# Attention and a mixture of experts on one core: the values before the transpositions in each steady turn

## The chip, the cores and the metric

The kernel runs on one core of a Trainium2 chip. The metric is the device time of one execution in microseconds. All computation is in one launch; nothing runs on other cores.

## What is computed

Eight batches of 128 tokens with 256 features pass through one block. Cut to what matters, the reference is:

```python
x = x + attention(layernorm(x), ctx, ctx, length)    # 8 batches, 8 * 16 = 128 "heads x 16" rows, see below
x = x + moe(layernorm(x))                            # 8 experts, capacity 128, plus a shared expert

def attention(q, k, v, length):      # q, k, v: (8, 128, 256); the 128 rows are 8 heads of 16
    s = SCALE * log(length)          # one factor for each batch
    attn = softmax(s * einsum('bhdq,bhdk->bhqk', q, k))
    return einsum('bhqk,bhdk->bhdq', attn, v)

def moe(x):                          # 1024 tokens
    probs = softmax(x @ Wg); e = argmax(probs); gate = probs[e]
    # the first 128 tokens of each expert in order are kept
    out = gate * ((silu(x @ W1[e]) * (x @ W3[e])) @ W2[e])
    return out + (silu(x @ sw1) * (x @ sw3)) @ sw2
```

## The kernel before

There are 64 heads in all, eight for each of eight batches. The attention runs as a software pipeline of "turns", t = 0 to 32 (STEADY = 33), written out by hand in the same order for each engine. Each engine executes its own list in order and waits on semaphores. A turn handles two heads.

TensorE's part of turn t was, before the change:

- **Values**, one half of a group (weigh_values, L1110). A group m is four heads. Its eight matmuls multiply the exponentials pt with the values vext and add into the PSUM bank O; half c=0 starts the sums, c=1 ends them and raises valued. Group m had its halves in turns 2m+10 and 2m+11. Two groups make a batch; the first half of a batch's first group waits for o_copied, as it overwrites O.
- **Scores** (L1070) of heads 2t and 2t+1, up to turn 31, whose row maxima VectorE takes (nm, L578), interleaved with **shifted scores** (L1094) of heads 2(t-7) and 2(t-7)+1. These are the scores again, transposed and with the maxima subtracted; ScalarE takes their exponentials (pt, L843). A score of head n waits for the maximum of head n-3, which has the same bank.
- **Transpositions**, at most one kind in a turn, through the bank X, which they share in a fixed order (x_free). In turns 4b+4 the maxima of batch b (turn_maxima, L1079); in turns 4b+14 the attention output of batch b from osum (turn_output, L1124), waiting for o_copied; in turns 4b+15 its way back after the division (turn_back, L1136), waiting for scaled; in turns 21, 25, 29 the normed tokens (turn_tokens, L1147).

From turn 12 on, there is a transposition in each turn save 13 and 17. Turns 12, 16, 20, 24, 28 and 32 have the maxima.

ScalarE in a turn: if it is turn 4b+13, copy_output (osum, L849: O to SBUF after valued, raises o_copied); then the first exponential; then, in turns 4b+4, maxima_rows (mrow, L836, waits for the maxima's transposition and lets SP reload them into qz by two small DMAs); or high_tokens (xhi, L859) after a token transposition; then the second exponential; then token_rstd (rstd, L855) of the second layer norm.

VectorE in a turn: two maxima (L578), then one of scale_output (rinv L586, att L591), add_attention (xs, L600), token statistics (st, L605) or low_tokens (xlo, L616). In turn 14 it also takes the statistics of the last two query batches (st, L535). GpSimd does the token norm (mrs L440, rk L443) after rstd and splits weights (L450 to L465). The expert splitting starts in turn 32 and is followed by token_norm(4).

Behind the loop the order is written out: half (11, 1) of the values, the shifted scores of heads 52 to 55, turn_tokens(3), values (12, 0), turn_output(5), values (12, 1), shifted scores of 56 to 59, turn_back(5), values 13, turn_tokens(4), shifted scores of 60 to 63, turn_output(6) and so on into the shared expert and the experts.

Of the kernel before, what the change touches and what calls it, by code (L numbers as in the profile page):

```python
# [46 lines left out]
NG = NH // 4  # L47
# [11 lines left out]
LAG = 7  # L59
# [27 lines left out]
END = TURNS + LAG  # L87


def turns(offset, *last):  # L90


    return [4 * b + offset for b in range(B - len(last))] + [END + n for n in last]
# [1 line left out]

WEIGH = [(2 * m + LAG + 3, 2 * m + LAG + 4) for m in range(NG - 1)] + [(END, END)]
OUT_COPY, OUT_TURN, OUT_SCALE = turns(LAG + 6, 1), turns(LAG + 7, 4), turns(LAG + 7, 5)
OUT_BACK, OUT_ADD = turns(LAG + 8, 6), turns(LAG + 8, 7)  # L100
SHIFTED = 5
# [17 lines left out]
def shifted_bank(n):  # L119

    return NS + n % NS if n < FOURS else FOURS_BANKS[(n - FOURS) % len(FOURS_BANKS)]


def banks_last_head(n):

    return next((k for k in range(n - 1, -1, -1) if shifted_bank(k) == shifted_bank(n)), None)
# [40 lines left out]
def block_kernel(nc, x, ctx_in, lens, wg, w1, w3, w2, sw1, sw3, sw2, consts, out):  # L167
    with ExitStack() as es:
# [148 lines left out]
        def ring_pass(n, size):  # L317

            return n // size + 1
# [687 lines left out]
        def _(pe):  # L1007
# [17 lines left out]
            def unread(t):  # L1025

                if t in (4, 6, 7):
                    pe.wait_ge(nm_row, 1)
                if t == 9:
                    pe.wait_ge(nm_row, 2)  # L1030
                unread_rows(UNREAD.get(t, 0))
# [3 lines left out]
            def turn_values(n):  # L1035

                if n == 0:
                    pe.wait_ge(ld_cst, 16)
                else:
                    pe.wait_ge(v_copied, n)  # L1040
                for b in range(2 * n, 2 * n + 2):
                    pe.wait_ge(ld_ctx[chunk_of[b]], 16)
                    for c in range(2):
                        k = 2 * (b % 2) + c
                        mm = nc.tensor.transpose(O[:, k * P:(k + 1) * P], cs[:, b, c * P:(c + 1) * P], ident)
                mm.then_inc(v_turned, 1)

            def place(n):

                b, i = divmod(n, H)  # L1050
                first = ROWS * (HEADS[i] // 2)
                return b, HEADS[i] % 2, slice(first, first + ROWS)

            def scores(n, u):

                b, half, rows = place(n)
                scores_bank = bank[n % (2 * NS) if n < FIRST else n % NS]
                if n % H == 0 and u == 0:
                    if b < EAGER:
                        pe.wait_ge(k_eager, 2 * b + 1)  # L1060
                        pe.wait_ge(q_eager, b + 1)
                    else:
                        pe.wait_ge(k_made, 2 * (b - EAGER + 1))
                        pe.wait_ge(q_made, 2 * (b + 1) - EAGER)
                if n % H == 2 and u == 0 and b < EAGER:
                    pe.wait_ge(k_eager, 2 * (b + 1))
                    pe.wait_ge(q_made, b + 1)
                if n >= 2 * NS and u == 0:
                    pe.wait_ge(maxed, n - 2 * NS + 1 if n < FIRST + NS else n - NS + 1)
                mm = nc.tensor.matmul(scores_bank[:, u * D:(u + 1) * D], qz[rows, b, half, u * P:(u + 1) * P],  # L1070
                                      kz[rows, b, half, :], start=True, stop=True)
                if u == 1:
                    mm.then_inc(scored, 1)

            def turn_maxima(b):
                pe.wait_ge(maxed, H * (b + 1))
                x_free("maxima", b)
                for u in range(2):
                    mm = nc.tensor.transpose(X[0:H, u * P:(u + 1) * P], nm[:, b % 2, u, :], ident)  # L1079
                mm.then_inc(nm_turned, 1)  # L1080

            def shifted_scores(n, c):

                b, half, rows = place(n)
                if n < NS and c == 0:
                    pe.wait_ge(maxed, FIRST - NS + n + 1)
                if n % H == 0 and c == 0:
                    pe.wait_ge(ld_m[b % 2], 32 * ring_pass(b, 2))
                last = banks_last_head(n)
                if last is not None and c == 0:  # L1090
                    pe.wait_ge(exped, last + 1)
                if n >= FOURS and shifted_bank(n) < NS and c == 0:
                    pe.wait_ge(maxed, NH)
                mm = nc.tensor.matmul(bank[shifted_bank(n)][:, c * D:(c + 1) * D], kz[rows, b, half, c * P:(c + 1) * P],  # L1094
                                      qz[rows, b, half, :], start=True, stop=True)
                if c == 1:
                    mm.then_inc(shifted, 1)

            def weigh_values(m, c):

                b, first = divmod(m, 2)
                pe.wait_ge(exped, 4 * m + 4)
                if m == 0:
                    pe.wait_ge(v_copied, B // 2)
                if first == 0 and b >= 1:
                    pe.wait_ge(o_copied, b)
                for i in range(4):
                    h = HEADS[4 * first + i]
                    g, j = divmod(h, 4)
                    mm = nc.tensor.matmul(O[32 * j:32 * j + 32, g * D:(g + 1) * D], vext[:, b, c, h, :],  # L1110
                                          pt[:, m % NPT, i, c * D:(c + 1) * D],
                                          start=(c == 0), stop=(c == 1), skip_group_check=True)
                if c == 1:
                    mm.then_inc(valued, 1)
# [92 lines left out]
                mm.then_inc(pos_done, 1)  # L1207

            for t in range(STEADY):
                for m in range(NG):  # L1210
                    for c in range(2):
                        if t == WEIGH[m][c]:
                            weigh_values(m, c)
                if t < LAG and t % 2 == 0:
                    first_half, heads = range(2), range(2 * t, min(2 * t + 4, 2 * LAG))
                    if t == 0:
                        for u in range(2):
                            for n in first_half:
                                scores(n, u)
                        heads = range(2, 4)  # L1220
                    for u in range(2):
                        for n in heads:
                            scores(n, u)
                for part in range(2):
                    for k in range(2):
                        if LAG <= t < TURNS:
                            scores(2 * t + k, part)
                        if 0 <= t - LAG < TURNS:
                            shifted_scores(2 * (t - LAG) + k, part)
                if t == MROW[0]:  # L1230
                    turn_maxima(0)
                if t in VALUES:
                    turn_values(VALUES.index(t))
                if t in UNREAD:
                    unread(t)
                for when, work in ((MROW[1:], turn_maxima), (OUT_TURN, turn_output), (OUT_BACK, turn_back),
                                     (TTURN, turn_tokens)):
                    if t in when:
                        work(when.index(t) + (1 if work is turn_maxima else 0))

            def four_shifted(n):

                for part in range(2):
                    for k in range(4):
                        shifted_scores(n + k, part)
# [77 lines left out]
                                          start=(c == 0), stop=(c == FC - 1))  # L1323
                mm.then_inc(e_down, 1)

            weigh_values(11, 1)
            four_shifted(52)
            turn_tokens(3)
            weigh_values(12, 0)
# [72 lines left out]
```

## Time and profile before

| | |
|---|---|
| median of 3 runs | 153.0 us (152.81 to 153.4) |
| the profiled execution | 153.0 us, span 151.1 us |
| mean granted clock of TensorE | 0.991 |
| busy, share of the span | TensorE 139.9 us (93%), VectorE 99.3 (66%), ScalarE 82.1 (54%), GpSimd 67.9 (45%) |
| scores L1070, shifted scores L1094, values L1110 | 34.6, 34.6, 19.8 us busy |

The span goes from the first to the last instruction; the rest of the time lies around it. Busy time counts overlapping matmuls once in the engine's total. The end of a matmul in the trace is modelled, so groups are best measured from start to start. A turn of the loop takes about 2 us, a cycle of four turns 8.2 us; the loop ends at about 71 us.

### The profile page before, as it was taken

What the parts mean: (1) busy time and instruction counts of PE and PEld (TensorE: products, weight loads), DVE (VectorE), ACT (ScalarE), POOL (GpSimd) and SP (SyncE); (2) the same over time, 40 slices, a digit from 0 to 9 for tenths busy, and PEclk for the clock granted to TensorE, in tenths of its full rate; (3) what the DMA queues carried; (4) which work ended last, traced back from release to release, by engine and by line L of the source; (5) the groups of instructions that cost most, each with busy time, mean ns of one, the idle gap of its engine ahead of it and who ended that gap; (6) DMA issues with size and microseconds to landing.
All of it is one profiled execution on the core that took longest, in us unless ns stands there. A gap on an engine that the chain in (4) does not pass through costs nothing.

```text
span 151.1 us, 3413 instructions
## 1 busy us (share of the span) xinstructions
PE 139.9 (93%) x1254; PEld 95.4 (63%) x1254; DVE 99.3 (66%) x232; ACT 82.1 (54%) x179; POOL 67.9 (45%) x100
## 2 busy tenths in 40 slices
PE   7799999998999999999887999999999999999930
PEld 2365564554554555554443677688999999999720
DVE  0589896778888888887225346877673487774220
ACT  3444275674858676776876357544503676662300
POOL 7116739401850506349992000276600588467250
PEclk9999999999999999999999999999999999999996
DMA  3993454444171700000530099722465622212110
GB/s 70 345 357 118 119 174 143 152 143 146 36 259 39 242 7 5 0 8 0 157 131 4 2 305 323 237 105 70 160 196 156 175 77 80 69 42 91 35 63 35
DMA packets 15825, 18.42 MB, mean 122 GB/s; under 512 B 1981, under 2 KB 15078, under 8 KB 15809
## 3 DMA queue, kind: packets, MB, share of 16 engines
q1 hardware_dynamic: 14368, 14.98, 31.5%
q0 software_dynamic: 1152, 2.97, 6.0%
q10 hardware_dynamic: 288, 0.26, 0.6%
q8 instruction: 10, 0.16, 0.5%
q14 instruction: 7, 0.05, 0.1%
HBM read 14.12 MB, written 4.21 MB: 121 GB/s over the span
## 4 chain that ended last, share of the span: by engine, by line
PE 83%; DVE 4%; DMA 4%; issue 3%; ACT 2%; POOL 1%; SPq 0%; ACTq 0%; POOLq 0%; DVEq 0%
PE bank L1070 20%; PE bank L1110 11%; PE bank L1321 6%; PE bank L1174 6%; PE bank L1175 6%; PE bank L1297 5%; PE bank L1296 5%; PE bank L1262 4%; PE bank L1094 4%; PE bank L1022 3%; PE bank L1124 3%; DMA xs<-in_x 2%; PE bank L1136 2%; PE bank L1079 2%; PE bank L1308 2%
## 5 line engine op out<-in xcount | busy, mean ns | idle before, releaser
L578 DVE TENSOR_REDUCE nm<-bank 128x2 f32<-128x512 f32 x64 | 40.9, 686 | 10.0 <-PE bank L1070 9.5
L843 ACT ACTIVATE pt<-bank 128x512 f32<-128x512 f32 x64 | 35.6, 597 | 17.4 <-PE bank L1094 17.3
L1070 PE MATMUL bank<-kz,qz 32*128 32x256 f32 x256 | 34.6, 400 | 0.9 <-DVE qz L555 0.9
L1094 PE MATMUL bank<-qz,kz 32*128 32x256 f32 x256 | 34.6, 400 | 0.0
L1070 PEld LDWEIGHTS bank<-kz,qz 32*128 32x128 f32 x256 | 21.9, 184 | 13.3 <-DVE nm L578 5.8
L1094 PEld LDWEIGHTS bank<-qz,kz 32*128 32x128 f32 x256 | 21.6, 184 | 1.7 <-ACT pt L843 1.0
L1110 PE MATMUL bank<-pt,vext 128*32 128x256 f32 x256 | 19.8, 390 | 0.1
L502 POOL DMA_INDIRECT expert_rows<-rk,idx_s x8 | 8.7, 1088 | 19.5 <-DVE idx_s L655 17.7
L415 POOL TENSOR_SCALAR qz<-xs,rs,mrs 128x256 f32<-128x256 f32 x14 | 7.7, 561 | 20.0 <-DVE mrs L549 20.0
L517 POOL DMA_INDIRECT xs<-out,rk x8 | 9.9, 1235 | 12.0 <-DMA out<-xs 9.8
L524 POOL DMA_INDIRECT out<-xs,rk x8 | 8.2, 1020 | 8.8 <-DVE xs L741 4.4
L1022 PE MATMUL bank<-onesb 128*128 128x512 bf16 x34 | 10.7, 452 | 1.0 <-POOL onesb L409 1.0
L1110 PEld LDWEIGHTS bank<-pt,vext 128*32 128x32 f32 x256 | 5.4, 108 | 6.8 <-issue 5.2
L440 POOL TENSOR_SCALAR mrs<-mv,rstd 128x1 f32<-128x1 f32 x6 | 1.6, 259 | 16.6 <-ACT rstd L855 16.6
L616 DVE TENSOR_TENSOR xlo<-bank,xhi 128x256 fp32r<-128x256 f32 x8 | 3.4, 421 | 7.0 <-ACT xhi L859 7.0
L465 POOL TENSOR_TENSOR ew<-wraw,ew 128x352 fp32r<-128x352 f32 x8 | 7.5, 932 | 0.7
L968 ACT ACTIVATE late<-bank 128x352 f32<-128x352 f32 x8 | 3.7, 464 | 7.3 <-PE bank L1297 7.3
L735 DVE TENSOR_TENSOR qz_rest<-bank,late 128x352 f32<-128x352 f32 x8 | 4.2, 520 | 5.1 <-ACT late L968 5.1
L1321 PE MATMUL bank<-wraw,kz_rest 128*128 128x256 f32 (+1 forms) x30 | 7.4, 381 | 0.0
L1022 PEld LDWEIGHTS bank<-onesb 128*128 128x128 bf16 x34 | 3.4, 112 | 5.9 <-issue 3.7
L1262 PE MATMUL bank<-shi,hThi 128*128 128x256 f32 (+1 forms) x24 | 7.0, 290 | 0.0
L1262 PE MATMUL bank<-shi,hTlo 128*128 128x256 f32 (+1 forms) x24 | 6.8, 282 | 0.0
(153 smaller groups left out, 301.1 us busy)
## 6 DMA issues: line engine op xcount, KB each, us to landing
wraw<-in_w SPq DMA_DIRECT2D x10, 352.0 KB, 3.4
wlate<-in_w SPq DMA_DIRECT2D x6, 352.0 KB, 4.4
wraw<-in_w SPq DMA_DIRECT2D x10, 128.0 KB, 3.5
expert_rows<-zero SPq DMA_DIRECT2D x1, 1032.0 KB, 6.7
out<-xs SPq DMA_DIRECT2D x8, 128.0 KB, 2.1
xs<-in_x SPq DMA_DIRECT2D x3, 256.0 KB, 5.1
cs<-in_ctx SPq DMA_DIRECT2D x3, 256.0 KB, 5.3
wlate<-in_w SPq DMA_DIRECT2D x6, 128.0 KB, 4.4
```

The costliest lines, as they stand in the source:

```text
L502: nc.gpsimd.indirect_dma_start(xd_dram, bass.IndirectOffsetOnAxis(ap=idx_s[:, b:b + 1], axis=0), x2[:, b, :], None, bounds_check=E * C - 1 ...
L517: nc.gpsimd.indirect_dma_start(res[:, e, :], None, out_rows, number(e), bounds_check=B * P - 1, oob_is_err=False).then_inc(gathered[e], 16)
L578: nc.vector.tensor_reduce(nm[:, b % 2, :, place], scores_bank[:].rearrange("p (u c) -> p u c", u=2), AX_X, ALU.max, negate=True).then_inc( ...
L843: nc.scalar.activation(pt[:, g % NPT, n % 4, :], bank[shifted_bank(n)][:], ACT.Exp).then_inc(exped, 1)
L1022: nc.tensor.matmul(X[:].rearrange("p (n c) -> p n c", c=P), onesb[:], onesb[:].unsqueeze(1).broadcast_to([P, 4, P]), start=True, stop=True)
L1070: mm = nc.tensor.matmul(scores_bank[:, u * D:(u + 1) * D], qz[rows, b, half, u * P:(u + 1) * P], kz[rows, b, half, :], start=True, stop=True)
L1094: mm = nc.tensor.matmul(bank[shifted_bank(n)][:, c * D:(c + 1) * D], kz[rows, b, half, c * P:(c + 1) * P], qz[rows, b, half, :], start=Tru ...
L1110: mm = nc.tensor.matmul(O[32 * j:32 * j + 32, g * D:(g + 1) * D], vext[:, b, c, h, :], pt[:, m % NPT, i, c * D:(c + 1) * D], start=(c == 0 ...
L1174: nc.tensor.matmul(u1, weights(part, S1 + f * P, F + WG, c, n1), tokens, start=a, stop=z)
L1175: mm = nc.tensor.matmul(u3, weights(part, S3 + f * P, F, c, n3), tokens, start=a, stop=z)
L1262: mm = nc.tensor.matmul(base_bank[b % 2][:, 0:D], hpart[0:rows, half, f, j * P:(j + 1) * P], part[0:rows, S2 + f * D:S2 + (f + 1) * D], st ...
L1321: mm = nc.tensor.matmul(y_bank[(e + 1) % 2][:, 0:D], hTe[0:rows, e % 2, c * P:(c + 1) * P], down_at[e][c][0:rows], start=(c == 0), stop=(c ...
```

## The change

The half of the values stands behind the scores of a turn and ahead of its transposition, in place of ahead of the scores. Its turn is one earlier: group m has its halves in turns 2m+9 and 2m+10. In the stream of TensorE's instructions each half so changes places with the transposition (and, in turn 9, with the two unread matmuls) that stood ahead of it. Group 11's second half moves from behind the loop into turn 32. The program of every other engine stays as it is.

```diff
-WEIGH = [(2 * m + LAG + 3, 2 * m + LAG + 4) for m in range(NG - 1)] + [(END, END)]
+WEIGH = [(2 * m + LAG + 2, 2 * m + LAG + 3) for m in range(NG - 4)]
@@
             for t in range(STEADY):
-                for m in range(NG):
-                    for c in range(2):
-                        if t == WEIGH[m][c]:
-                            weigh_values(m, c)
                 if t < LAG and t % 2 == 0:
...
                             scores(2 * t + k, part)
                         if 0 <= t - LAG < TURNS:
                             shifted_scores(2 * (t - LAG) + k, part)
+                for m, halves in enumerate(WEIGH):
+                    for c in range(2):
+                        if t == halves[c]:
+                            weigh_values(m, c)
                 if t == MROW[0]:
                     turn_maxima(0)
@@
-            weigh_values(11, 1)
             four_shifted(52)
             turn_tokens(3)
```

## Rows read from the trace of the kernel before

**Rows 1.** The page, chain that ended last, share of the span by engine.
```profile
PE 83%; DVE 4%; DMA 4%; issue 3%; ACT 2%; POOL 1%; SPq 0%; ACTq 0%; POOLq 0%; DVEq 0%
```

**Rows 2.** Windows: length, busy us of PE, PEld, DVE, ACT, POOL, granted clock, DMA.
```profile
45.64:53.86 8.22, 8.22 (x111) 4.44 (x108) 6.93 (x14) 5.70 (x13) 2.23 (x4) 1.00 0.40 132
...
70.28:83.81 13.53, 11.46 (x142) 5.83 (x141) 5.12 (x15) 10.51 (x26) 9.30 (x15) 1.00 0.25 82
```

**Rows 3.** Timeline of TensorE, turns 20 to 22: start us, length us, what.
```profile
45.64 0.38 PE L1079 MATMUL bank<-cst,nm 128*8 128x128 f32 x2
45.95 0.64 PE L1110 MATMUL bank<-pt,vext 128*32 128x256 f32 x8
46.52 0.48 PE L1070 MATMUL bank<-kz,qz 32*128 32x256 f32 x1
...
47.60 0.44 PE L1147 MATMUL bank<-cst,rk 128*128 128x128 f32 x2
47.97 0.64 PE L1110 MATMUL bank<-pt,vext 128*32 128x256 f32 x8
```

**Rows 4.** Timeline of ScalarE in the same turns.
```profile
46.26 0.34 ACT L836 COPY mrow<-bank 8x256 f32<-8x256 f32 x1
46.51 0.58 ACT L843 ACTIVATE pt<-bank 128x512 f32<-128x512 f32 x1
47.00 0.56 ACT L849 COPY osum<-bank 128x512 f32<-128x512 f32 x1
```

**Rows 5.** Timeline of all engines, turn 4.
```profile
13.59 0.39 PE L1079 MATMUL bank<-cst,nm 128*8 128x128 f32 x2
...
14.01 0.36 ACT L836 COPY mrow<-bank 8x256 f32<-8x256 f32 x1 [1.77 <-PE bank L1079]
```

**Rows 6.** Timeline of all engines, from turn 13 into turn 14.
```profile
29.79 0.48 PE L1070 MATMUL bank<-kz,qz 32*128 32x256 f32 x1
...
30.27 0.56 ACT L849 COPY osum<-bank 128x512 f32<-128x512 f32 x1
...
30.97 0.42 PE L1110 MATMUL bank<-pt,vext 128*32 128x256 f32 x4
```

**Rows 7.** Timeline of VectorE, turn 14.
```profile
32.70 1.29 DVE L578 TENSOR_REDUCE nm<-bank 128x2 f32<-128x512 f32 x2 [0.46 <-PE bank L1070]
33.91 0.74 DVE L535 BATCH_NORM_STATS2 st<-xs 128x6 f32<-128x256 f32 x2
```

**Rows 8.** Timeline of all engines, turn 15.
```profile
35.04 0.42 DVE L591 TENSOR_TENSOR att<-bank,rinv 128x256 f32<-128x256 f32 x1
...
35.39 1.28 DVE L578 TENSOR_REDUCE nm<-bank 128x2 f32<-128x512 f32 x2
...
35.52 0.44 PE L1136 MATMUL bank<-cst,att 128*128 128x128 f32 x2 [0.46 <-DVE att L591]
...
36.46 0.48 PE L1070 MATMUL bank<-kz,qz 32*128 32x256 f32 x1
```

**Rows 9.** Timeline of all engines, start of turn 18.
```profile
40.17 0.48 PE L1070 MATMUL bank<-kz,qz 32*128 32x256 f32 x1
...
40.33 0.48 PE L1070 MATMUL bank<-kz,qz 32*128 32x256 f32 x1
```

**Rows 10.** Timeline of all engines, behind the loop.
```profile
71.61 0.56 ACT L849 COPY osum<-bank 128x512 f32<-128x512 f32 x1
...
72.82 0.37 ACT L859 CAST xhi<-bank 128x256 fp32r<-128x256 f32 x1
...
73.22 0.42 DVE L616 TENSOR_TENSOR xlo<-bank,xhi 128x256 fp32r<-128x256 f32 x1 [1.91 <-ACT xhi L859]
```

**Rows 11.** Timeline of all engines, token norms of GpSimd and who waits.
```profile
66.04 0.26 POOL L440 TENSOR_SCALAR mrs<-mv,rstd 128x1 f32<-128x1 f32 x1 [4.32 <-ACT rstd L855]
...
77.95 0.44 PE L1147 MATMUL bank<-cst,rk 128*128 128x128 f32 x2 [0.51 <-POOL rk L443]
```

**Rows 12.** The page, DMA issues: KB each, median us to landing.
```profile
out<-xs SPq DMA_DIRECT2D x8, 128.0 KB, 2.1
```

## The prediction

> **What bounds the kernel now.** I read four views in this order. The chain that ended last is mostly TensorE [rows 1], so the question is where TensorE waits. The windows over a cycle of four turns show it busy without a gap (8.22 of 8.22 us, turns 20 to 23), while ScalarE has 5.70 us of work there and VectorE 6.93 [rows 2]. In the stretch behind the loop it idles 2.07 of 13.53 us. TensorE's timeline gives the length of each group of a turn from start to start: scores 1.08 us (46.52 to 47.60), maxima 0.31, values 0.57, token transposition 0.37 [rows 3]. These lengths add up in any order: values follow directly on scores in turns 9 to 12 now, at the same 0.57. So swapping groups that never wait is worth nothing. What can move the time is a wait that appears or goes. ScalarE's timeline of the same turns shows the order that matters: mrow (row of maxima), an exponential, then osum (the copy of O), back to back [rows 4].
>
> **What moves.** No instruction, semaphore or DMA is added or removed. Each half of the values in turns 10 to 32 moves ahead of the transpositions in the turn before it. So in every turn with a transposition, that transposition starts 0.57 us later against the scores, and the values start earlier by its length.
>
> **The new wait.** turn_maxima (L1079) runs in turns 4b+12. The second half of group 2b+1 used to follow it and now precedes it. Freeing it early doesn't help: copy_output(b) stands in ScalarE's program behind maxima_rows and one exponential, and maxima_rows waits for the transposition. The next values, group 2b+2, restart O and wait for that copy (o_copied). They used to come after the next scores and that turn's transposition; now they come right after the scores. With M the end of the maxima's transposition:
> - mrow starts at M+0.02 (13.98 to 14.01 in turn 4, where ScalarE had nothing else) [rows 5]. Now it is held until 46.26 by the exponential before it, though M is 46.02.
> - From there 0.25 to the exponential and 0.49 to osum, whose length is 0.56 [rows 4]. It ends at M+1.32.
> - osum's end at 30.83 releases values at 30.97, so 0.14 more [rows 6]: M+1.46.
> - TensorE starts the next scores at M-0.07 (fill and drain overlap: 45.95 against 46.02) and is through with them at M+1.01 [rows 3].
>
> So it waits 0.45 us. Both ends: if the exponential is not in the way or the restart overlaps, 0.30; if transfer times are longer, 0.60. I take 0.45, worked from the nearest rows. Behind the waiting values stand the turn's transposition and the next scores, so VectorE and ScalarE starve with it; neither is late by itself, since each had slack.
>
> **The sum, turn by turn.** Turns 9 to 12 keep their times (no transposition before the maxima of turn 12).
> - Turn 13: wait 0.45, against one of 0.10 now, since turn 13 has no transposition and values start at 30.97 where scores end 1.08 after 29.79. +0.35.
> - Turn 14: now the second head of the scores waits for VectorE's reduction of the turn before, a stagger of 0.16 as in turn 18 (40.17 to 40.33 [rows 9]). The later turn hides it. -0.16, running +0.19.
> - Turn 15: here the swap pays. TensorE idles 0.46 before turn_back(0) [rows 8], which follows VectorE's chain of two maxima, statistics and att that starts with 32.70 [rows 7]. That chain starts 0.36 later, so turn_back goes at 35.88; but the values, 0.57 us, are now done before it. The scores of turn 16 start at 36.25 instead of 36.46. Running -0.21.
> - Turn 16: VectorE is late next. Its pair of maxima from 35.39 [rows 8] moves to 35.75, the first is free after 0.61 and 0.14 more, 36.50. Stagger 0.25, running +0.04.
> - Turn 17: as turn 13, +0.35. Turn 18: stagger gone, -0.16. Running +0.23.
> - Turns 21, 25, 29: these now have a token transposition (0.37) that covers the copy, so the whole 0.45 is new. +1.36, running +1.6 us.
> - Behind the loop ScalarE's order is mrow, exponential, osum, exponential, xhi. It starts at the later M: osum 71.99 instead of 71.61 on the old clock, xhi 72.99 instead of 72.82, then xlo (73.22) and turn_output(5) [rows 10]. +0.17.
>
> Sum +1.77 us. Two covers to check. The reload of the maxima through SP starts 0.35 us later against the turn and is due three turns on, about 4 us after mrow; the SP copies of the outputs land in 2.1 us [rows 12]. Price nothing; only a landing above 4 us would count. GpSimd's token norm waits for rstd [rows 11], whose cause, xhi, is late by 0.57 more than the 0.29 that TensorE's wait and drain already give, so its splitting of expert weights starts about 2.0 us late. turn_tokens(4) waits 0.51 us for it now (77.95) [rows 11] and comes about 0.2 later than the rest, but turn_output(6) waits for ScalarE's chain of osum(6), rstd, an exponential and xhi(4), so that is absorbed. Lost cover would cost 0.2 us. From there everything hangs in one chain on TensorE, so the shift reaches the end.
>
> The profiled execution took 153.0 us with a span of 151.1, the median is also 153.0. 151.1 + 1.8 + 1.9 around the span gives 154.8 us.
>
> **A rule against the row.** The new waits start with a weight load. In the row, TensorE begins again only behind the wait: the values start 0.14 after osum's end [rows 6], and their group of eight then takes the full 0.64, fill included. The Trainium skill (TensorE: Matmul & The Clock Gate, Architectural detail) says that the queue can pull weight loads ahead of matmuls in flight. By it the first load would be done in the wait, and each of five restarts would save the fill of 0.07 at most, for 154.4 us; the rows show no such thing after a semaphore wait. The sum goes by the rows.
>
> **Rivals.**
> - Not slower (0.10): the copy of O is in time. Then the wait of turns 13 to 29 is 0 and only the hidden stall of turns 15 and 16 counts. By the same steps the scores of turn 16 end 0.3 us earlier, and the late VectorE keeps it there: 152.7 us. For it speaks that valued now comes earlier, when ScalarE is idle half of some turns. It decides where osum ends before M+0.87, 0.45 earlier than I work out; against it speaks ScalarE's fixed order [rows 4].
> - Order costs (0.06): transpositions between values and scores lose the overlap of 0.07 that each change of group has now, in 19 turns: +1.3, 156.1 us. The groups behind the loop, values into turn_back, show no such loss.
> - Clock (0.02): the granted clock is 1.00 in the cycles and also in the stretch with 2.07 us of idle [rows 2], the upper of the two levels (2.4 GHz). If five new gaps brought it down to 1.2 GHz, a turn of 2.05 us of TensorE work would take up to twice as long, and five such turns cost 10 us: 165 us. The page named above has this rule under A second HAM failure mode: frequent micro-idles between groups of matmuls let the clock swing. No row here shows it, the wait of 0.46 before turn_back(0) included.
> - Something unseen that leaves the time where it was (0.02).
>
> **The numbers.** My forecast has 0.80. Its own range follows from the wait's ends, five times 0.15 either way: 154.0 to 155.6. The range for 8 in 10 reaches to the neighbours: 153.5 to 156.0. Within 0.5% (0.77 us, about what a measurement tells from no change) lie 0.07 of the first rival, 0.02 of my own low end and the unseen 0.02; faster by more is 0.03 of the first rival, should the tail gain as well. Slower: 0.78 + 0.06 + 0.02, so 0.86.
>
> **What would show it.** Right: TensorE idle of some 0.4 us before values (L1110) in turns 13, 17, 21, 25 and 29, with osum (L849) as releaser or just ended; the 0.46 before L1136 in turn 15 shrunk to 0.1; cycles of 8.67 instead of 8.22 us; the stretch behind the loop longer by 0.2. Wrong: cycles of 8.2 (the copy is in time), waits before L1079, L1136 or L1147 in the steady turns (transpositions late in themselves), waits before L1094 for the reload, or a granted clock under 1.00.

## The result and the profile after

The changed kernel takes 154.91 us in the median (154.82 to 155.06, 4 runs), the kernel before 153.09 us (4 runs); the ratio is 1.0121, 95% interval 1.0109 to 1.0133. The change makes the kernel 1.2% slower. The profiled execution has a span of 153.0 us, 1.9 more than before, with a granted clock of 0.986.

First, three rows of the changed kernel's waits, of TensorE's matmuls alone (engine, what waited, for whom: us in total, times, longest us):

```profile
PE bank L1110 <- ACT osum L849: 2.1, 5, 0.4
...
PE bank L1147 <- POOL rk L443: 0.8, 1, 0.8
...
PE bank L1147 <- DVE xs L600: 0.6, 1, 0.6
```

The page's chain, which answers to [rows 1], passes less through TensorE and more through ScalarE and GpSimd:

```profile
PE 76%; POOL 8%; ACT 5%; issue 4%; DMA 2%; DVE 1%; SPq 0%; ACTq 0%; POOLq 0%; DVEq 0%
```

Of the waits, the first row has no counterpart before the change: five waits of TensorE for the copy of O, 2.1 us together. The other two are behind the loop and were there before (0.51 and 0.61 us). The last one has not grown. Now TensorE's timeline in turns 20 to 22, which answers to [rows 3], and ScalarE's, which answers to [rows 4]:

```profile
45.81 0.64 PE L1110 MATMUL bank<-pt,vext 128*32 128x256 f32 x8
46.38 0.38 PE L1079 MATMUL bank<-cst,nm 128*8 128x128 f32 x2
46.70 0.48 PE L1070 MATMUL bank<-kz,qz 32*128 32x256 f32 x1
...
48.26 0.64 PE L1110 MATMUL bank<-pt,vext 128*32 128x256 f32 x8 [0.42 <-ACT osum L849]
48.83 0.44 PE L1147 MATMUL bank<-cst,rk 128*128 128x128 f32 x2
```

```profile
46.80 0.36 ACT L836 COPY mrow<-bank 8x256 f32<-8x256 f32 x1 [0.26 <-PE bank L1079]
47.07 0.58 ACT L843 ACTIVATE pt<-bank 128x512 f32<-128x512 f32 x1
47.56 0.56 ACT L849 COPY osum<-bank 128x512 f32<-128x512 f32 x1
```

Read the two together. The values of turn 20 are through at 46.45, yet osum, which needs only them, starts at 47.56. ScalarE first sits idle for 0.26 us waiting for the maxima's transposition, which ends at 46.76. mrow follows at 46.80, then an exponential, then osum. osum ends at 48.12 and the values start 0.14 later. TensorE's list has nothing else that it may do. The same row with the same 0.42 stands at 31.26, 39.92, 56.97 and 65.67 (turns 13, 17, 25, 29).

The windows of one cycle show what this costs, and that the work is the same (columns as in [rows 2]):

```profile
45.50:54.20 8.70, 8.28 (x111) 4.46 (x106) 7.01 (x15) 5.71 (x13) 2.23 (x4) 1.00 0.38 124
54.20:62.90 8.70, 8.28 (x110) 4.45 (x106) 7.01 (x15) 5.71 (x13) 3.23 (x6) 1.00 0.01 3
```

A cycle of four turns has become 8.70 us instead of 8.22, at the upper clock level throughout.

Turn 15 is where the swap pays. TensorE's timeline, answering to [rows 8]:

```profile
35.13 0.64 PE L1110 MATMUL bank<-pt,vext 128*32 128x256 f32 x8
35.81 0.44 PE L1136 MATMUL bank<-cst,att 128*128 128x128 f32 x2
36.18 0.48 PE L1070 MATMUL bank<-kz,qz 32*128 32x256 f32 x1
...
36.41 0.48 PE L1070 MATMUL bank<-kz,qz 32*128 32x256 f32 x1
```

turn_back(0) still waits for att, but 0.11 us from start to start (35.13 and 0.57 for the values make 35.70; it starts at 35.81). Before the change the same reckoning gives 0.52 (33.92 and 1.08 make 35.00; it starts at 35.52 [rows 8]). The values fill the time. The stagger in turn 16, the time by which the second head's scores start behind the first head's (36.18 to 36.41), takes back 0.23.

Behind the loop, all engines, answering to [rows 10] and [rows 11]:

```profile
73.67 0.56 ACT L849 COPY osum<-bank 128x512 f32<-128x512 f32 x1
...
74.62 0.34 ACT L859 CAST xhi<-bank 128x256 fp32r<-128x256 f32 x1
...
75.00 0.42 DVE L616 TENSOR_TENSOR xlo<-bank,xhi 128x256 fp32r<-128x256 f32 x1 [2.04 <-ACT xhi L859]
...
80.02 0.44 PE L1147 MATMUL bank<-cst,rk 128*128 128x128 f32 x2 [0.81 <-POOL rk L443]
...
81.64 0.63 PE L1124 MATMUL bank<-cst,osum 128*128 128x128 f32 x4
```

turn_output(5) starts at 75.57, where it started at 73.79 before. Ahead of it, values (12, 0) start 0.49 us after turn_tokens(3) (73.88 to 74.37) instead of 0.37, as they too need O copied; turn_output(5) waits longer than that for xlo, so this costs nothing by itself.

How the delay grows, from the starts of the same group in both timelines. The changed kernel's profiled execution enters turn 12 0.10 us earlier (it is as early already at the first scores, 6.83 against 6.92 us, long before the change), so 0.10 is added to each difference.

| start of | before | after | delay + 0.10 | by the prediction |
|---|---|---|---|---|
| scores of turn 14 | 31.54 | 31.83 | 0.39 | 0.35 |
| scores of turn 16 | 36.46 | 36.18 | -0.18 | -0.21 |
| scores of turn 17 | 38.42 | 38.36 | 0.04 | 0.04 |
| scores of turn 18 | 40.17 | 40.49 | 0.42 | 0.39 |
| scores of turn 19 | 42.55 | 42.72 | 0.27 | 0.23 |
| scores of turn 30 | 64.97 | 66.61 | 1.74 | 1.60 |
| shifted scores of head 52 | 71.16 | 72.80 | 1.74 | 1.60 |
| shared expert, first matmul | 83.81 | 85.59 | 1.88 | 1.77 |

From the last row to the end of the span the changed kernel takes 67.41 us and the kernel before 67.29. These 0.12 us were not traced to a cause; they happen to make up for the 0.10 of the start, so the spans differ by 1.9 as well.

### The profile page after: what moved, and what is told of

Read it like the earlier page. It is cut to its first block, busy times and chain, and to the rows that moved or that the text cites. A ratio compares the mean times of both kernels' runs of the same rounds, so it can differ in the third digit from the quotient of the medians.

```text
span 153.0 us, 3413 instructions
## 1 busy us (share of the span) xinstructions
PE 140.4 (92%) x1254; PEld 95.5 (62%) x1254; DVE 99.6 (65%) x232; ACT 82.2 (54%) x179; POOL 67.5 (44%) x100
## 4 chain that ended last, share of the span: by engine, by line
PE 76%; POOL 8%; ACT 5%; issue 4%; DMA 2%; DVE 1%; SPq 0%; ACTq 0%; POOLq 0%; DVEq 0%
PE bank L1070 16%; PE bank L1110 9%; PE bank L1321 6%; PE bank L1174 6%; PE bank L1262 6%; PE bank L1175 5%; PE bank L1296 5%; PE bank L1297 5%; POOL ew L465 4%; PE bank L1022 3%; DMA xs<-in_x 2%; PE bank L1124 2%; ACT pt L843 2%; POOL ew L463 2%; PE bank L1094 2%
## 5 line engine op out<-in xcount | busy, mean ns | idle before, releaser
L465 POOL TENSOR_TENSOR ew<-wraw,ew 128x352 fp32r<-128x352 f32 x8 | 7.5, 933 | 0.7
L1262 PE MATMUL bank<-slo,hThi 128*128 128x256 f32 (+1 forms) x24 | 6.8, 282 | 0.0
```

The lines of the kernel that those rows point to most:

```text
L465: nc.gpsimd.tensor_tensor(elo[e][:, a:z], whole[e][:, a:z], ehi[e][:, a:z].bitcast(F32), ALU.subtract).then_inc(ew_lo_pool, 1)
L1262: mm = nc.tensor.matmul(base_bank[b % 2][:, 0:D], hpart[0:rows, half, f, j * P:(j + 1) * P], part[0:rows, S2 + f * D:S2 + (f + 1) * D], st ...
```

## The experiments

Each ratio is against the kernel before the change, run on the same chip in the same rounds. The first four ran on one chip. The maxima first, ScalarE's best order on the kernel before and the two with the statistics ran on a second, where the kernel before scattered from 153.04 to 154.10 us; this widens their intervals. GpSimd's norm and both gains at once ran on a third, the copy first on the kernel before on a fourth. Many of the differences here are as small as the intervals. Where a timeline is compared instead, starts are counted from the scores of turn 12 (27.83 before the change, 27.73 after it).

**ScalarE's copy ahead of mrow.** TensorE's list is that of the changed kernel; the copy leaves the start of the next turn for the maxima turn itself.

```diff
-                if t in OUT_COPY:
-                    copy_output(OUT_COPY.index(t))
                 if 0 <= t - LAG < TURNS:
                     exponentials(2 * (t - LAG))
+                if t in MROW[2:]:
+                    copy_output(MROW.index(t) - 2)
                 if t in MROW[1:]:
                     maxima_rows(MROW.index(t))
```

> The changed kernel, with ScalarE's copy of O (osum) taken in the maxima turn itself, between the first exponential and mrow, in place of behind mrow and the second exponential. TensorE's list is untouched. Theory (the copy is late because it stands behind mrow and an exponential): the wait of 0.42 us before the values in turns 13, 17, 21, 25, 29 disappears as a wait on osum; the values then wait at most for the second exponential, which now comes last, about 0.1 us. With the gain in turn 15 kept, 153.1 us, and no more than 153.5. Rival (transpositions that start 0.57 us later cost by themselves, whatever ScalarE's order): stays at 154.5 or above.

Measured: 153.11 us, ratio 1.0001 (0.9992 to 1.0010). The time is that of the kernel before, with the transpositions exactly as late as in the changed kernel. The row of waits on osum has gone. Its timeline of TensorE in turns 20, 21 and 24 (L1109 is the values here):

```profile
45.42 0.64 PE L1109 MATMUL bank<-pt,vext 128*32 128x256 f32 x8
...
47.51 0.64 PE L1109 MATMUL bank<-pt,vext 128*32 128x256 f32 x8
...
53.77 0.64 PE L1109 MATMUL bank<-pt,vext 128*32 128x256 f32 x8
```

A cycle between values (45.42 to 53.77) is 8.35 us, which leaves 0.13 over the 8.22 of before: the second exponential is last now. So the even result is a balance: counted from turn 12 (27.94 here) the scores of turn 17 (38.20) are 0.33 us earlier than before the change, by turn 15, and three cycles of 0.13 take it back.

**The copy, the exponential, then mrow.** As above, with maxima_rows moved behind the second exponential.

> The changed kernel with ScalarE's order first exponential, osum, second exponential, mrow. Theory: no wait before the values in any of the five turns (the second exponential is through 0.3 us before TensorE comes), and 152.8 us, provided that the reload of the maxima through SP, which starts about 0.65 us later than in the changed kernel, still lands within about 3 us. If it doesn't, TensorE waits before the shifted scores (L1094) of turns 15, 19, 23, 27, and the time is above 153.5. Rival (late transpositions cost by themselves): 154.5 or above.

Measured: 152.70 us, ratio 0.9972 (0.9962 to 0.9982). It has the lowest ratio of all versions, though the interval of the statistics one turn earlier, below, overlaps it. Its timeline of TensorE (the source is shorter by one line, so L1109 is the values, L1135 turn_back, L1069 the scores) shows turn 13 into 14 and turn 15:

```profile
30.93 0.64 PE L1109 MATMUL bank<-pt,vext 128*32 128x256 f32 x8
...
35.06 0.64 PE L1109 MATMUL bank<-pt,vext 128*32 128x256 f32 x8
35.63 0.44 PE L1135 MATMUL bank<-cst,att 128*128 128x128 f32 x2
36.00 0.48 PE L1069 MATMUL bank<-kz,qz 32*128 32x256 f32 x1
```

No wait is left before the values, and none before turn_back. Cycles are 8.22 again (values at 45.25, 53.47, 61.69). So the reload landed in time, though mrow came later. The gain of 0.4 us comes from turn 15 alone. Counted from turn 12 (27.90 here), the scores of turn 15 start as late as before the change, since the 0.1 us that turn 13 gives comes back as a longer stagger in turn 14 (31.50 to 31.77). The scores of turn 16 start 0.53 earlier and those of turn 17 0.46. Behind the loop turn_tokens(3) waits 0.2 us for mrow (it starts at 72.05, 1.28 us after the shifted scores, which take 1.075), so turn_output(5) is only 0.38 us earlier than before the change.

**The swap in the maxima turns alone.** The loop over WEIGH stands ahead of the transpositions under `if t in MROW` and behind them under `if t not in MROW`.

> The changed kernel with the values ahead of the transposition in the maxima turns alone (12, 16, 20, 24, 28, 32); in all other turns the values stand behind the transposition again, as before the change. Theory: osum comes just as late (1.3 us after the maxima's transposition ends), but in turns 21, 25 and 29 the token transposition of 0.37 us covers most of it; left are about 0.1 us there, 0.42 in turns 13 and 17, and the hidden stall of turn 15 is back. Worked out the same way, 154.1 us. Rival (each of the 19 swapped turns costs a little): only 6 of them are swapped, so about a third of the loss, 153.7 us or less, and no wait on osum longer than now.

Measured: 154.13 us, ratio 1.0077 (1.0063 to 1.0091). The waits are two on osum of 0.42 us each, and turn 15's stall is back:

```profile
31.43 0.64 PE L1110 MATMUL bank<-pt,vext 128*32 128x256 f32 x8 [0.42 <-ACT osum L849]
...
35.98 0.44 PE L1136 MATMUL bank<-cst,att 128*128 128x128 f32 x2 [0.60 <-DVE att L591]
...
40.44 0.64 PE L1110 MATMUL bank<-pt,vext 128*32 128x256 f32 x8 [0.42 <-ACT osum L849]
...
48.29 0.44 PE L1147 MATMUL bank<-cst,rk 128*128 128x128 f32 x2
48.78 0.64 PE L1110 MATMUL bank<-pt,vext 128*32 128x256 f32 x8
```

In turn 21 the token transposition stands in the gap again (48.29), and the values follow 0.49 later instead of 0.37: the cover leaves 0.12 of the wait of 0.49 that the changed kernel has from start to start.

**The copy behind one more exponential.** The reverse of the first: copy_output stands behind the first exponential of its turn.

> The changed kernel with osum put behind one more exponential, the first of the next turn, which can only start 1.14 us after the maxima's transposition ends. Theory: the values start 0.14 us after osum ends, so the wait of 0.42 grows to about 1.3 us in each of the five turns; nothing else covers it: +4.4 us, 159.3 us (158.5 to 160). Rival (the waits on osum only take the place of other stalls, and the loss is elsewhere): less than half of that, below 157 us.

Measured: 159.27 us, ratio 1.0407 (1.0392 to 1.0421). The waits:

```profile
PE bank L1110 <- ACT osum L849: 6.4, 5, 1.3
```

4.3 us more wait gives 4.4 us more time: what TensorE waits here reaches the end in full.

**The maxima ahead of the values again.** In turns 12, 16, ..., 32 the old order, elsewhere the new one.

```diff
+                if t in MROW[2:]:
+                    turn_maxima(MROW.index(t))
                 for m, halves in enumerate(WEIGH):
...
-                for when, work in ((MROW[1:], turn_maxima), (OUT_TURN, turn_output), (OUT_BACK, turn_back),
+                for when, work in ((MROW[1:2], turn_maxima), (OUT_TURN, turn_output), (OUT_BACK, turn_back),
```

> The changed kernel with the maxima's transposition ahead of the values again in turns 12, 16, ..., 32; all other turns keep the new order. Theory: mrow is no longer late against osum, so the wait on osum falls from 0.42 to the 0.1 us that turn 13 had before the change, now in all five turns (turns 21, 25 and 29 lost the cover of the token transposition). The gain in turn 15 shrinks, since the maxima of turn 16 then wait for VectorE's add. Sum against the kernel before: -0.13 + 3 x 0.10, so 153.3 us (153.0 to 153.5). Rival (late transpositions of the output, its way back and the tokens cost by themselves): 154 or above.

Measured: 153.57 us beside 153.40, ratio 1.0006 (0.9987 to 1.0024). In its trace no wait on osum is named any more; from start to start 0.1 us is left before the values of turns 13, 21, 25 and 29, as expected (29.84 and 1.075 make 30.92, and the values of turn 13 start at 31.02). The maxima of turn 16 do wait for VectorE's add:

```profile
31.02 0.64 PE L1110 MATMUL bank<-pt,vext 128*32 128x256 f32 x8
...
35.61 0.44 PE L1136 MATMUL bank<-cst,att 128*128 128x128 f32 x2
...
37.46 0.38 PE L1079 MATMUL bank<-cst,nm 128*8 128x128 f32 x2 [0.16 <-DVE xs L600]
```

Output, its way back and the tokens are as late as in the changed kernel, at no price that can be measured: counted from turn 12 (27.88 here) the shifted scores of head 52 (71.41) are 0.20 us later than before the change, and 0.17 was expected. The loss needs the maxima's transposition behind the values.

**ScalarE's best order on the kernel before.** The same order, exponential, osum, exponential, mrow, with TensorE's old list.

> The kernel before the change, with ScalarE's order first exponential, osum, second exponential, mrow, as in the fastest kernel so far. Theory: here TensorE's values of turn 13 still stand behind the maxima, so osum ends no earlier than about 1.6 us after the scores and the second exponential about 2.0, which leaves the wait of 0.1 us in turns 13 and 17 and cover in the others; the stall of 0.5 us in turn 15 stays. No change: 153.1 us (152.9 to 153.4). Rival (the ScalarE order alone made the gain of the fastest kernel): 152.7 us.

Measured: 155.80 us, ratio 1.0132 (1.0102 to 1.0163). Both theories missed; it is 2 us slower. The trace names the cause (L1146 is turn_tokens here):

```profile
48.42 0.41 PE L1146 MATMUL bank<-cst,rk 128*128 128x128 f32 x2 [0.45 <-ACT mrow L836]
```

```profile
PE bank L1146 <- ACT mrow L836: 1.8, 4, 0.5
```

The maxima and the tokens share the bank X, so turn_tokens waits until mrow has read it. Four of these waits make 1.8 of the 2.0 us. I had followed mrow only to the reload three turns on, not to the next user of its bank. In the changed kernel's steady turns the values stand ahead of the tokens and cover this; behind the loop they don't, which is the 0.2 us seen above.

**The same with mrow ahead of the second exponential,** again on the kernel before:

> The kernel before the change, with ScalarE's order first exponential, osum, mrow, second exponential. It differs from the last try on this kernel only in that mrow stands ahead of the second exponential. There turn_tokens waited 0.45 us for mrow in turns 21, 25, 29 and behind the loop, since mrow frees the bank X that they share. Theory: with mrow 0.5 us earlier this wait is at most 0.1 us, so 153.1 to 153.4 us, or within 0.3% of the kernel before. Rival (osum ahead of mrow costs here in another way): 154.5 or above, as most of the 2.0 us stays.

Measured: 153.88 us beside 153.12, ratio 1.0051 (1.0037 to 1.0065). That is outside the 0.3% expected, though far from the rival. No wait on mrow is named any more, and 1.2 of the 2.0 us are gone, less than the 1.8 of those waits, as a new wait has come that I had not priced: in turns 13 and 17, with no token transposition, the values now wait for the second exponential, which comes last.

```profile
31.39 0.64 PE L1109 MATMUL bank<-pt,vext 128*32 128x256 f32 x8 [0.37 <-ACT pt L843]
```

Turn 13's values start 2.08 us after turn 12's (29.31 to 31.39), where the kernel before had 1.75 (29.22 to 30.97 [rows 6]). The same 0.33 comes in turn 17, and the stagger of turn 18 that goes with it gives 0.15 back. Counted from turn 12 (27.92 here), the scores of turn 19 are 0.52 us later than before the change, those of turn 22 0.58, and turn_output(5) 0.89; the time says 0.8. So the gain of 152.70 us belongs to both orders together; either alone loses.

**The statistics one turn earlier,** once on the kernel before and once on the changed one. This prices turn 15's stall by itself.

```diff
-LATE = {2: 3, 3: 7, 4: 14}
+LATE = {2: 3, 3: 7, 4: 13}
```

> The kernel before the change, with the last two batches' query statistics (1.0 us of VectorE) one turn earlier, in turn 13 in place of 14. Theory: this alone removes the stall of turn 15, since att then is ready 0.5 us earlier; 152.6 us (152.4 to 152.8). Rival (the stall of turn 15 is not worth its length, as the next stagger takes it back): 153.0 or above.

Measured: 153.12 beside 153.40, ratio 0.9977 (0.9956 to 0.9998), a gain of 0.35 us, whose interval (0.03 to 0.67) also holds the 0.5 of the theory. The trace is sharper: it shows 0.24, and says why: LATE moves query_rstd in ScalarE's list too, which waits for the statistics in turn 14 and holds the exponentials of heads 14 and 15 back from 32.75, their start in the kernel before, to 33.58. By the kernel's waits that makes the shifted scores of head 17 late, which need the bank of head 14; turn_back(0) starts at 35.27, and the scores of turn 16 at 36.21 instead of 36.46 (turn 12 at 27.82 and 27.83).

> The changed kernel with the same move of the statistics from turn 14 to 13. Theory: the changed kernel already covers the stall of turn 15 with values and is left with 0.1 us there and a stagger of 0.23 in turn 16; so the move is worth only 0.3 us, 154.6 us, and the loss by the change grows from 1.8 to 2.0 us. Rival (the swap in turn 15 gained nothing): the move is worth 0.5 us here too, 154.4 or less.

Measured: 155.28 us, ratio 1.0115 (1.0076 to 1.0154), beside 1.0121 of the changed kernel alone. The time can't tell 0.1 from 0.3 us here. The trace shows the stagger of turn 16 gone (scores at 36.25 and 36.27) and the values of turn 16 0.27 us earlier against those of turn 12 (28.94 to 37.33, where the changed kernel has 28.81 to 37.47). That is near the 0.3 of the theory and not the 0.5 of the rival. But on the kernel before the same move gave 0.24 in its trace, so the pair doesn't tell whether the swap gained in turn 15. The table above does: between the scores of turns 15 and 16 the changed kernel takes 2.12 us (34.06 to 36.18), the kernel before 2.54 (33.92 to 36.46).

**GpSimd's token norm earlier.** In the changed kernel token_norm(4) moves one split of weights (1.4 us) ahead.

> The changed kernel with GpSimd's token_norm(4) one split of expert weights (1.4 us) earlier behind the loop. TensorE waits 0.81 us for it before turn_tokens(4) in the changed kernel, 0.51 before the change. Theory (turn_output(6) waits for ScalarE's chain osum, rstd, exponential, xhi anyway): that wait goes from 0.81 to nearly nothing but comes back before turn_output(6), and the time stays at 154.9 us (at most 0.1 less). Rival (GpSimd's lateness of 2.1 us is a part of the loss): 154.6 us or less.

Measured: 155.12 us, ratio 1.0114 (1.0088 to 1.0141), beside 1.0121 of the changed kernel; the interval alone would allow a gain of up to 0.5 us. The trace shows none: from the scores of turn 12 to the shared expert's first matmul it takes 57.85 us (27.94 to 85.79), the changed kernel 57.86. The wait moves as expected, from turn_tokens(4) to turn_output(6) (lines are one further here):

```profile
79.35 0.44 PE L1148 MATMUL bank<-cst,rk 128*128 128x128 f32 x2
79.71 1.15 PE L1095 MATMUL bank<-qz,kz 32*128 32x256 f32 x16
81.84 0.63 PE L1125 MATMUL bank<-cst,osum 128*128 128x128 f32 x4 [0.98 <-DVE xlo L617]
```

0.81 us at one place has become 0.98 at another. The chain of the page gives GpSimd 8% of the changed kernel's span (4% of it the splitting, L465), and still it is worth nothing: in the changed kernel turn_output(6) already starts 1.25 us after the shifted scores ahead of it (80.39 to 81.64), which take 1.08, so ScalarE's chain ends last even there.

**Both gains at once:** ScalarE's best order and the statistics in turn 13, on the changed kernel.

> The changed kernel with ScalarE's order exponential, osum, exponential, mrow, and with the statistics in turn 13. Each was worth something alone; here both at once. In the first the stall of turn 15 is already covered and only a stagger of 0.1 to 0.2 in turn 16 is left, so 152.6 us (152.4 to 152.8). Rival (the gains add up): 152.2 us.

Measured: 153.08 us beside 153.18, ratio 0.9990 (0.9963 to 1.0017). This is slower than expected, and the gains don't add. The interval overlaps that of ScalarE's best order alone, so the time doesn't show that the statistics take something back. The traces do. Both have the scores of turn 12 at 27.90; those of turn 16 start at 36.28 here and at 36.00 without the move, and from turn 17 on all starts are 0.21 us later. The exponentials of heads 14 and 15 again stand behind query_rstd, until 33.66.

## Why the prediction was right

It forecast 154.8 us; measured were 154.91.

- **The new wait** is where and what it was said to be. Its mechanism is shown from both sides: osum ahead of mrow removes the loss, osum later enlarges it by what the wait grows, the old place of the maxima alone removes it. The size was 0.45 and is 0.485 from start to start (46.70 to 48.26 less 1.075). The difference is ScalarE's path, counted from M, the end of the maxima's transposition: mrow starts at M+0.04 and the next exponential 0.27 behind it instead of 0.25, as ScalarE stands waiting here and was busy in [rows 4]. The prediction has M+0.02, but its own row, 13.98 to 14.01, gives 0.03. Five times 0.03 is the 0.14 us by which the sum is short at the end of the loop; 0.03 less behind it leaves 0.11. That the forecast time came within 0.1 us is in part luck, since the 0.10 us at the start and the 0.12 at the end, of the profiled executions, which the prediction did not treat, cancel.
- **Turns 14 to 18**, the staggers that go and come and the 0.4 us gained in turn 15, came out within 0.04 us each (table).
- **The cover in turns 21, 25, 29** is shown by the swap in the maxima turns alone: two waits of 0.42 and three remainders of 0.12.
- **Behind the loop**, +0.17 forecast, 0.14 found; osum's start moved from [rows 10] to 73.67. GpSimd's norm starts 2.07 us late (68.11 against 66.04 [rows 11]) and the splitting behind it as much, or 2.17 with the 0.10 of the table; 2.0 was said. Its lateness is absorbed, as the experiment confirms.
- **The restart** after a wait brought no saving from an early weight load: from osum's end to the first matmul it is 0.14 to 0.15 in all five waits, as in [rows 6], and the group takes its full 0.64. In turn 21 the first weight load starts at 48.23, 0.11 after osum's end and 0.03 ahead of the matmul, not within the wait. So the rule cited from the Trainium skill (TensorE: Matmul & The Clock Gate, Architectural detail), that the queue can pull weight loads ahead of matmuls in flight, changed nothing here.
- **The rivals.** "In time" failed on ScalarE's fixed order. Lost overlap between values, transposition and scores does not exist: 45.81, 46.38, 46.70 are the same 0.57 and 0.31 as before, within 0.01. The clock stayed at its upper level: the granted clock is 1.00 in every stretch from turn 12 to the end of the loop.

The weaker point is what the forecast did not look at: who else waits for mrow. It did no harm in the changed kernel, but it spoiled a later expectation by 2 us.

## What to carry to other kernels

When two groups of a busy engine change places, price not the groups but the other engines' lists: a step freed earlier is worth nothing if it is queued behind a step that you have just made later. Follow each copy that is moved to every waiter, the next user of its buffer as well as the reader of its result. And move both lists together: here the new order of TensorE and the new order of ScalarE lose 1.8 and 2.0 us alone and gain 0.4 together.

## What was not expected of the hardware

The short copies of ScalarE cost slightly more when the engine stood waiting for them. mrow takes 0.36 us after an idle stretch and 0.34 behind a running instruction, and the next instruction starts 0.27 instead of 0.25 behind it (46.80 and 47.07 against [rows 4]). The same 0.27 and 0.25 stand behind xhi (49.31 to 49.58 after a wait, 48.22 to 48.47 without one in the kernel before), though its own length is 0.37 both times.
